# Query stacks by a DMA round trip, maxima of four heads by one matmul, and one maximum over two PSUM banks

## The reference, cut to what matters

```python
q = (query @ Wq.T + bq).reshape(B, Sq, H, Hd).transpose(0, 2, 1, 3)   # 8 x 16 heads x 112 x 16
k = (key @ Wk.T + bk).reshape(B, Skv, H, Hd).transpose(0, 2, 1, 3)    # 8 x 16 heads x 375 x 16
v = (value @ Wv.T + bv).reshape(B, Skv, H, Hd).transpose(0, 2, 1, 3)
q = q * SCALE
scores = jnp.einsum('bhqd,bhkd->bhqk', q, k)
attn = jax.nn.softmax(scores, axis=-1)
out = jnp.einsum('bhqk,bhkd->bhqd', attn, v)
out = out.transpose(0, 2, 1, 3).reshape(B, Sq, D)
return out @ Wo.T + bo
```

## Time and profile before

| | before |
|---|---|
| median of 3 runs | 648.78 us (646.63 to 649.30) |
| the profiled execution, its own time | 643.75 us |
| its span in the profile | 641.9 us |
| TensorE busy in the span | 420.9 us (66%) |
| VectorE | 433.1 us (67%) |
| ScalarE | 264.8 us (41%) |
| GpSimd | 110.0 us (17%) |
| mean granted clock of TensorE | 0.795 of 2.4 GHz |
| attention loop in the span | about 293 to 447 us |

### The profile page before, as it was taken

How to read it: one execution, slowest core, us unless ns; L and a number is a source line. 1 busy time by engine, 2 the same in 40 slices (tenths; PEclk the granted TensorE clock), 3 DMA queues, 4 the chain that set the end, 5 groups by cost and what they waited for, 6 DMA issues and landing times.

```text
span 641.9 us, 10182 instructions
## 1 busy us (share of the span) xinstructions
PE 420.9 (66%) x3448; PEld 301.2 (47%) x3448; DVE 433.1 (67%) x1714; ACT 264.8 (41%) x627; POOL 110.0 (17%) x209
## 2 busy tenths in 40 slices
PE   2998799623393303557888888899999655406306
PEld 2667685511273103444666665677555553106303
DVE  4645999899746796958886775775454575473573
ACT  4744544812303541015454553665543452351340
POOL 7900000000042891525810000000000000000000
PEclk9997699655585755569898998999999887855556
DMA  4560004292007992001699895700200271000002
GB/s 134 155 159 1 2 2 155 72 200 76 2 1 113 135 137 19 1 0 36 182 114 182 127 215 52 74 1 2 104 28 1 79 256 59 2 0 1 1 1 58
DMA packets 45769, 47.16 MB, mean 73 GB/s; under 512 B 5197, under 2 KB 43926, under 8 KB 44694
## 3 DMA queue, kind: packets, MB, share of 16 engines
q1 hardware_dynamic: 45718, 46.51, 35.3%
HBM read 37.80 MB, written 8.60 MB: 72 GB/s over the span
## 4 chain that ended last, share of the span: by engine, by line
PE 52%; DVE 25%; ACT 9%; issue 6%; SPq 3%; POOL 3%; DMA 2%; DVEq 0%; ACTq 0%
PE ps L1958 7%; PE ps L1912 4%; DVE PR L982 4%; ACT below L1593 4%; PE ps L1899 4%; PE ps L1734 3%; PE ps L1888 3%; PE ps L1742 3%; SPq L548 3%; PE ps L1798 3%; PE ps L1874 2%; PE ps L2084 2%; DMA ctxP<-in_ctx 2%; POOL ct L744 2%; DVE prod L978 2%
## 5 line engine op out<-in xcount | busy, mean ns | idle before, releaser
L1143 DVE TENSOR_REDUCE negm<-ps 112x1 f32<-112x375 f32 x128 | 65.8, 543 | 18.8 <-PE ps L1888 15.7
L1564 ACT ACTIVATE E<-ps 125x448 f32<-125x448 f32 x96 | 52.0, 544 | 59.4 <-PE ps L1899 59.3
L1888 PE MATMUL ps<-ks,qs 96*112 96x375 bf16 x128 | 44.0, 353 | 14.6 <-issue 10.6
L2057 PE MATMUL ps<-cnt,same 128*128 128x3 bf16 (+4 forms) x40 | 6.8, 170 | 61.8 <-ACT below L1593 43.4
L1912 PE MATMUL ps<-E,v 125*32 125x112 f32 x768 | 42.8, 274 | 0.0
L1899 PE MATMUL ps<-qs,ks 99*125 99x112 bf16 x384 | 40.1, 228 | 1.6 <-DVE qs L1164 1.0
L1131 DVE TENSOR_REDUCE acts<-gel 128x4 f32<-128x448 f32 x32 | 19.8, 620 | 29.3 <-ACT gel L1527 29.3
L1899 PEld LDWEIGHTS ps<-qs,ks 99*125 99x125 bf16 x384 | 34.5, 140 | 10.4 <-issue 6.3
L727 POOL CAST kp<-kx 128x750 bf16<-128x750 f32 x8 | 6.5, 811 | 167.5 <-ACT path L1479 142.1
L2057 PEld LDWEIGHTS ps<-cnt,same 128*128 128x128 bf16 (+1 forms) x40 | 4.3, 109 | 65.0 <-issue 65.0
L1527 ACT ACTIVATE gel<-ps 128x448 f32<-128x448 f32 x32 | 17.3, 544 | 29.3 <-PE ps L1958 29.3
(11 more groups left out here) (363 smaller groups left out, 1133.4 us busy)
## 6 DMA issues: line engine op xcount, KB each, us to landing
ks<-key_parts SPq DMA_DIRECT2D x48, 187.5 KB, 8.5
piw<-fn_process_input_weights SPq DMA_DIRECT2D x8, 1024.0 KB, 4.9
key_parts<-kp SPq DMA_DIRECT2D x16, 281.2 KB, 4.7
ctx_again<-in_ctx SPq DMA_DIRECT2D x7, 512.0 KB
ctxP<-in_ctx SPq DMA_DIRECT2D x8, 375.0 KB
keys<-kx SPq DMA_DIRECT2D x16, 187.5 KB, 2.1
kx<-keys SPq DMA_DIRECT2D x8, 375.0 KB, 6.7
patn<-in_L_ffn_input_patterns SPq DMA_DIRECT2D x1, 2048.0 KB, 17.9
```

Source lines behind the costliest of these rows:

```text
L1143: drain(dve.tensor_reduce(negm[:, n:n + 1], bank(nm)[0:S, 0:SC], AX.X, ALU.max, negate=True), nm)
L1564: drain(fn(E[:, (KCH * f + c) % 6, :], bank(nm)[0:KC, 0:4 * S], ACT.Exp), nm)
L1888: fill(mm(bank(nm)[0:S, 0:SC], qs[0:SR, u // 4 % 3, n, :], ks[0:SR, u // 4 % 3, n, :], start=True, stop=True), nm)
```

## The change

1. The query stacks are no longer gathered by TensorE, but for batch 0 (four `queries`, now in banks 4 and 5). The split queries go to DRAM (`query_parts`, four stores) and come back as stacks in two halves of four batches, each by six DMAs of 16 partitions x 16 heads: 336 columns for half 0 (its first batch is left out), 448 columns for half 1. SyncE issues them between `load_stack(2)` and `store_parts(3)`. `qs` is now two tensors that hold all batches; the second lies over `qx32` and part of `qp`, so its load waits until both are read.
2. The negated maxima of four heads are transposed by one matmul into 12 rows. Under the keys of each head lie 12 rows (`kones`) with ones in its own three and zeros in the others. ScalarE, not VectorE, copies the rows, once for each of four heads by a broadcast. The matmuls behind have 108 rows instead of 99.
3. Scores for the maximum are made in pairs over two banks (0 and 1, 2 and 3), and VectorE takes two maxima by one instruction over 2 x 375 values.
4. GpSimd writes `kones` (a memset and two selects over 12 x 1500 values) once `joinF` and `joinG` are filled, and its 66 small memsets of `steps` come behind that. The small tensor `onesb` goes away, and `o` shares the place of `actscr`.

```diff
-        if 0 <= f + LAG + 1 < 4 * B:
-            p.add(("qstack", f + LAG + 1), 3)
+        if 0 <= f + LAG + 1 < 4:
+            p.add(("qstack", f + LAG + 1), 4 + (f + LAG + 1) % 2)
         if 0 <= f + LAG < 4 * B:
-            for i in range(4):
-                p.add(("smax", f + LAG, i), (4 * (f + LAG) + i) % 3)
+            for i in range(2):
+                p.add(("smax", f + LAG, i), 2 * i, 2 * i + 1)
...
         (SyncE, ahead of store_parts(3))
+            for half in range(2):
+                for t in range(2):
+                    sp.wait_ge(q_split, 2 * half + t + 1)
+                    sp.dma_start(query_parts[half, :, 128 * t:128 * t + 128, :].rearrange("c p s -> p c s"),
+                                 qp[:, t, :, 448 * half:448 * half + 448]).then_inc(queries_stored[half], 16)
+            for half in range(2):
+                sp.wait_ge(queries_stored[half], 32)
+                if half == 1:
+                    sp.wait_ge(queries_stored[0], 32)
+                    wait_filled(sp, ("qstack", 3))
+                lo = S if half == 0 else 0
+                for j, part in enumerate(Q_PARTS):
+                    sp.dma_start(qs[half][HD * j:HD * j + HD, :, lo:HB * S],
+                                 query_parts[half, part, :, lo:HB * S].rearrange("(n d) s -> d n s", d=HD)
+                                 ).then_inc(loaded[f"q{half}"], 16)
...
         (GpSimd, behind meet_ready)
+            wait_filled(pool, "joinF")
+            wait_filled(pool, "joinG")
+            did(pool.memset(kones[:, :, :], 1.0))
+            settle()
+            did(pool.affine_select(out=kones[:, :, :], in_=kones[:, :, :], compare_op=ALU.is_ge, fill=0.0, base=0,
+                                   pattern=[[-3, 4], [0, SC]], channel_multiplier=1))
+            settle()
+            pool.affine_select(out=kones[:, :, :], in_=kones[:, :, :], compare_op=ALU.is_ge, fill=0.0, base=2,
+                               pattern=[[3, 4], [0, SC]], channel_multiplier=-1).then_inc(kones_ready, 1)
...
         (VectorE)
-                        drain(dve.tensor_reduce(negm[:, n:n + 1], bank(nm)[0:S, 0:SC], AX.X, ALU.max, negate=True), nm)
+                        n = 4 * (u % 4) + 2 * i
+                        drain(dve.tensor_reduce(negm[:, n:n + 2], psum[0:S, 2 * i:2 * i + 2, 0:SC], AX.X, ALU.max,
+                                                negate=True), nm)
...
-                        drain(dve.tensor_copy(qs[SR:SR + 3, (f + 1) // 4 % 3, n:n + 4, :].rearrange("p n s -> p (n s)"),
-                                              bank(nm)[SR:SR + 3, 0:4 * S]), nm)
...
         (ScalarE)
+                    if c == 2 and 0 <= f + 1 < 4 * B:
+                        nm = ("negT", f + 1)
+                        wait_filled(act, nm)
+                        n = 4 * ((f + 1) % 4)
+                        drain(fn(queries_of(f + 1, slice(n, n + 4))[SR:SR + MR],
+                                 bank(nm)[SR:SR + MR, 0:S].unsqueeze(1).broadcast_to([MR, 4, S]), ACT.Copy), nm)
...
         (TensorE, scores_for_maximum)
+                    if u == 4:
+                        pe.wait_ge(loaded["q0"], 16 * len(Q_PARTS))
+                    if u == 4 * HB:
+                        pe.wait_ge(loaded["q1"], 16 * len(Q_PARTS))
...
         (TensorE, maxima)
-                for i in range(4):
-                    ins = mm(bank(nm)[SR:SR + 3, S * i:S * i + S], negp[:, f // 4 % 2, 4 * (f % 4) + i, :],
-                             identb[0:S, 0:S], start=True, stop=True)
+                fill(mm(bank(nm)[SR:SR + MR, 0:S], negp[:, f // 4 % 2, n:n + 4, :].rearrange("p n c -> p (n c)"),
+                        identb[0:S, 0:S], start=True, stop=True), nm)
```

More of the change, by code:

```diff
@@ L330, in build_program @@
         meet = [rd.take(f"meet{d}", [128, KB, 128]) for d in range(2)]
+        kones = Region(rd.at - 2 * 4 * KB * 128).take("kones", [MR, 4, SC], BF16)
         scratch = Region(rw.at + 4 * CT * B * D)
@@ L376, in build_program @@
         rs = rt.take("rs", [S, NH])
-        o = rt.take("o", [S, NH, HD])
+        o = actscr[0:S, :].rearrange("p (n e) -> p n e", n=NH)
         oT = rt.take("oT", [128, DH, S])
@@ L478, in bankb @@
             return ps[plan[name].banks[0]][:, :].bitcast(BF16)
-        names = ("x",) + tuple(f"ctx{b}" for b in range(B)) + ("again", "ones_k", "attnW", "ffnW", "small", "biasT", "pat", "oiw",
+        names = ("x",) + tuple(f"ctx{b}" for b in range(B)) + ("again", "ones_k", "q0", "q1", "attnW", "ffnW", "small", "biasT", "pat", "oiw",
                  "opat", "pval", "piw0", "piw1")
@@ L494, in build_program @@
              "pmx_ready pmd_ready pexp_ready vec scl pol").split()]
+        queries_stored = [sem(f"queries_stored{i}") for i in range(2)]
+        kones_ready = sem("kones_ready")
         parts_stored = [sem(f"parts_stored{i}") for i in range(2)]
@@ L648, in _ @@
                 did(pool.memset(t[:, :], 0.0))
-            for t in (ones, same[0], same[1], onesb):
+            for t in (ones, same[0], same[1]):
                 did(pool.memset(t[:, :], 1.0))
@@ L1152, in _ @@
                                  ALU.mult), nm)
-                    if i == 1 and b >= 0 and t == 3:
+                    if i == 0 and b >= 0 and t == 3:
                         nm = ("wo", b)
@@ L1185, in _ @@
                 if u < 4 * B and u % 4 == 3:
-                    for i in range(3):
-                        wait_drained(dve, ("smax", u, i + 1))
+                    for i in range(2):
+                        wait_drained(dve, ("smax", u, i))
                     part = negp[:, u // 4 % 2, :, :]
@@ L1970, in _ @@
                     scores_less_maximum(f, 0)
-                if ahead:
-                    scores_for_maximum(f + LAG, 1)
                 if b >= 0 and t == 1:
@@ L1996, in _ @@
                     scores_less_maximum(f, 1)
+                if f + LAG + 1 < 4:
+                    queries(f + LAG + 1)
                 if ahead:
-                    scores_for_maximum(f + LAG, 2)
-                if f + LAG + 1 < 4 * B:
-                    queries(f + LAG + 1)
+                    scores_for_maximum(f + LAG, 1)
                 if 0 <= f + 1 < 4 * B:
@@ L2004, in _ @@
                     value_products(f - 1, 1)
-                if ahead:
-                    scores_for_maximum(f + LAG, 3)
                 if now:
@@ L2181 @@
     args.append(nc.dram_tensor("keys", (B, D, SC), F32, kind="Internal").ap())
+    args.append(nc.dram_tensor("query_parts", (2, 3, D, HB * S), BF16, kind="Internal").ap())
     build_program(nc, *args)
```

55 lines of the change are left out of this document (28 added, 27 removed).

## The result

The changed kernel takes 671.29 us (median of four executions, 662.49 to 679.68) against 647.7 us before; the ratio is 1.0285, with a 95% interval of 1.022 to 1.0349: **slower by about 18.5 us**. Executions of one kernel fall into a fast group and a slow one, which has the lower granted clock, and the ratios compare the fast ones, while the profile of the changed kernel (an execution of 679.68 us) and those of six experiments caught slow ones, so that the size of the loss is taken from the ratios and the profiles serve for order and cause.

A forecast was written before the change was run, and what follows sets the result against it. No engine bounds the whole kernel; in the attention loop TensorE waits for key-stack loads of 14 us. Query loads +18.0, circle -0.7, steps behind 23 -1.5 and join +1.0 sum to +16.8: from 648.78 to 665.6 us, range 657 to 672.

The forecast's parts named there:

- The chain keys 5, split 5, stack 3, step 7: Attention loop: key load, GpSimd split, key-stack load, TensorE step, each awaiting the last; step 7 at 356.9 instead of 338.9.
- The term of +18.0: Query loads ahead of keys 5 in SyncE's queue delay split 5, hence step 7: +18.0 us, ends +16 and +20.5.
- 107 GB/s for the query loads: Loads into sixteen partitions run at the key stacks' rate: 2.41 MB in 22.5 us, from 298 to 320.7.
- the rival at 650 us: Query loads run at the stores' rate, 323 GB/s; sum +1.6, 650 us, no change; chance 0.05.
- The new wait for half 0 at 310: Step -1, batch 1's first scores, waits for half 0's queries until about 310: 5 us or so, costing nothing.
- The circle, -0.7: Steps 7 to 23, where stack load and TensorE step await each other: -0.7 us, ends -6.0 and +0.3.
- steps behind 23, -1.5: Loop steps from 23 on: -2.3 for less work, +0.7 for a cold start; -1.5 us, ends -3.0 and 0.
- the price of a restart step: Steps 7 to 23, from a wait's end to the next load issue: 4.65 us expected, from 5.63 at half clock.
- the 4.9 of the upper bound: Steps 7 to 23: all four restart steps at 4.9 us, the slow end of that term, +0.3 us.
- every restart at half clock: Steps 7 to 23: with waits of about 4 us every restart is at half clock; four give 18.6 against 19.3 us.
- The join, +1: GpSimd's memset, selects and small memsets slow VectorE at the start of the alignment walk: +1 us, bounds 0 to +4.
- the sum of +16.8: Whole kernel: 18.0 - 0.7 - 1.5 + 1.0 = +16.8 us, median to 665.6 us.

The follow-up runs named there:

- the runs with ScalarE's queue: Changed kernel with query loads issued by ScalarE: 661.75 us; with selecting columns made behind the walk and unread matmuls at the queries' wait 659.67, at every long wait 657.07.
- the round trip alone: Kernel before with only the queries' stores to DRAM and loads back as stacks added: 663.86 us, ratio 1.0277.
- columns late: Changed kernel with GpSimd making the selecting columns behind the walk instead of at the join: 667.06 us, ratio 1.0305.
- the fillers at two waits: Changed kernel with matmuls nobody reads ahead of TensorE's two long waits, 26 for the queries and 70 for stack 3: 670.64 us, ratio 1.034.
- fillers everywhere: Changed kernel with matmuls nobody reads ahead of every long wait of TensorE in the loop: 668.51 us, ratio 1.0308.

## Why the prediction was right, and where not

The forecast was 665.6 us and slower; the ratio of 1.0285 on 647.7 is 666.2 us. By its steps:

*The chain keys 5, split 5, stack 3, step 7: right.* Split 5 was forecast at 325.5 and started at 325.78; stack 3 at 342.4 and 342.11; step 7 at 356.9 and 356.62. The step came 17.7 us later, but 1.6 of these are the later start of split 3, behind the join, which had a term of its own. The term of +18.0 itself measures 16.1, its lower end; that the places agree to 0.3 us is in part luck. The reason was right for the changed kernel. That the bytes matter also when they are not ahead in the queue, the runs with ScalarE's queue show: there 6.0 to 8.7 of the 16.1 us stay.

*107 GB/s for the query loads: near, and 11% too low.* The four stores were issued by 298.98 and landed some 2.4 us behind their issue, and the first store of key parts was issued at 306.28; between them only query loads were under way. The stretches of the kernel after:

```profile
302.00:306.20 4.20, 1.81 (x15) 0.75 (x12) 3.98 (x6) 1.18 (x3) 4.00 (x4) 1.00 1.22 120
...
310.00:320.00 10.00, 9.43 (x64) 5.77 (x65) 5.54 (x6) 4.76 (x9) 0.00 (x0) 0.50 1.16 123
320.00:326.00 6.00, 6.00 (x55) 3.72 (x54) 3.11 (x7) 2.27 (x5) 0.22 (x1) 0.50 1.09 269
```

Up to 320 the engines moved 120 to 123 GB/s, although stores and loads of keys were queued from 306.28 on; from 320 on, 269, as those went through. That is far from the 323 of the stores, and the rival at 650 us fell with it. The prediction had 95 to 120 GB/s for the ends of this term, and +16 for its fast end. Of the Trainium skill's two rules the port count ("SBUF — State Buffer", Door 1: The DMA port swizzle) comes much the nearer, an estimate of 109 GB/s beside the measured 120. That the two differ was a wrong reading: the table with the 341 GB/s is for loads into 128 partitions.

*The new wait for half 0 at 310: right in its place (310.29), and wrong in that it cost nothing.* As time it was hidden. But the granted clock went to 0.50 with it and stayed there to step 7, and in the run without half 1's loads TensorE came to step 7 only 0.56 us ahead of stack 3.

*The circle, -0.7, and steps behind 23, -1.5: wrong in size and sign.* From step 7's start to the first pattern product it took 109.2 us before (338.88 to 448.1). With the round trip alone it is 113.3 (354.45 to 467.7), with the change but for the columns at the join 116.7 (355.22 to 471.9): +4 to +7.5, where the sum had -2.2. The changed kernel's own profile has 124.2, but caught the longest of its executions. Two things in the working failed.

The first is the price of a restart step. The prediction took 5.63 us for one at half clock, and expected 4.65 with fewer matmuls. But the mean clock in that row was 0.71, so only a part of the step had run at the lower level. At 0.50 throughout, the shorter step took 6.05 us (356.62 to 362.67). In the two experiments just named it took 5.84 us (columns late, mean clock 0.54) and 5.49 (round trip alone, 0.60, with the four transposes still in it). All are beyond the 4.9 of the upper bound.

The second is "every restart at half clock" as the whole of the clock's cost, with nothing for the steps behind. In the kernel before, each dip ended within some 5 us. In the changed one the clock stayed at 0.50 for about 26 us behind 356.62 and again behind 397.40, with every matmul of some steps at its slower duration. But in three experiments (the two just named and the fillers at two waits) the wait ahead of step 7, of 13 to 15 us, had a dip of only 3.5 to 6 us behind it. What makes a dip long stays open.

There is also a slip in the sum: three steps of 0.74 and five of 0.15 us make 3.0 and not 2.3, so the term behind step 23 would have been -2.3 by its own parts.

*The join, +1: too low at its place, +2.6,* within the bounds 0 to +4. Which operations would be hit was wrong for the most part: of L969 and L971 only the first was, by 0.31 us; 1.02 and 1.27 us fell on a tensor-tensor operation on one column and the operation behind it.

So the sum of +16.8 came near the measured 18.5 with some luck, by errors that offset each other. The chain was put too high (18.0 for 16.1, and 16.5 to 17.5 in the two experiments), the join too low (1.0 for 2.6), and the rest too low by 6 to 10 us (-2.2 for +4 to +7.5). The terms measured make 23 to 26 us, more than the ratio's 18.5; the profiled execution of before was 4 us faster than the median of its kernel, and the up to 4 us left over stay open.

## What to carry to other kernels

Before a DMA is put into a queue, ask what stands behind it: ahead of the one load on which a chain of dependent loads hangs, 2.41 MB of loads put off the chain by 16 us, though the instructions it saved were real. Another queue is a partial cure: 6 to 9 of these 16 us stayed. Work taken from an engine that waits for loads anyway may be worth nothing, here a ratio of 0.9993 for one matmul in place of four, and a longer wait can also take TensorE's clock, as the idle stretch ahead of 310 us did. A price read from a stretch holds for the mean clock of that stretch: look at it before calling it the price at half clock. And ask who had the PSUM bank that a saving needs.

## What the hardware showed that I had not expected

- In the kernel before TensorE's granted clock was back at 1.00 within some 5 us behind each wait; in the changed one it stood at 0.50 for about 26 us on end in which TensorE was never idle (19.38 of the first 19.40 us busy). Idle time ahead of 310 us is shown as the cause of the first such stretch, by the fillers. For the stretch behind 357 it isn't: with fillers everywhere it came after 46 us at 1.00 and a wait of 1.87 us. Nor does the length of the wait decide: behind 13.04 us the clock was back after 3.5 us. What does decide stays open. The Trainium skill's page "TensorE: Matmul & The Clock Gate" (Part 1) has the clock rise soon after the array is busy again: the kernel before agrees, these stretches don't.
- A filler matmul of 375 columns was issued every 160 ns at full clock (70 in 11.35 us), and 22 took 6.25 us at half.
- Loads spread over the queues of SyncE and ScalarE moved 231 GB/s where the same loads in one queue moved 144. It was one execution, and the mix of transfers wasn't the same: the query loads, into sixteen partitions each, moved 120 GB/s while nothing else was under way.
- Two GpSimd instructions of 1.5 us on 12 partitions stretched VectorE operations of 0.16 and 0.27 us to 1.18 and 1.54, until GpSimd's, begun at 117.52 and 119.07, were over. "SBUF — State Buffer" in the Trainium skill (SBUF: two separate sides) lets a VectorE operation with two SBUF inputs wait for a GpSimd operation that reads SBUF, and the rows agree; the prediction had looked at another pair of operations, of which one, L1003 now, took 0.56 us instead of 0.25 beside GpSimd's small memsets.
